# A four-layer graph network on one core: the third layer's gather pass as a pipeline of pairs of tiles

## The reference

```python
h = h_dir * h_mag                                  # one row of 256 per node
scores = h[src] @ a_s + h[tgt] @ a_t               # one number per edge
mx = maximum(segment_max(scores, tgt), -1e9)
ex = exp(scores - mx[tgt]);  se = segment_sum(ex, tgt)
agg = segment_sum(h[src] * (ex / (se[tgt] + 1e-10)), tgt)
```

## Time and profile before

| what | us |
|---|---|
| median of 3 runs | 4127.81 (4125.18 to 4128.53) |
| span of the profiled execution, first to last instruction | 4145.4 |
| the third layer's gather pass, first gather to last addition | 1642.65 to 2325.15 |

### The profile page before, as it was taken

How to read it: one execution, slowest core, us unless ns; L and a number is a source line. 1 busy time by engine, 2 the same in 40 slices (tenths; PEclk the granted TensorE clock), 3 DMA queues, 4 the chain that set the end, 5 groups by cost and what they waited for, 6 DMA issues and landing times. The chain is left out here.

```text
span 4145.4 us, 56575 instructions
## 1 busy us (share of the span) xinstructions
PE 2931.3 (71%) x12389; PEld 2013.0 (49%) x12389; DVE 2921.6 (70%) x6934; ACT 1927.7 (47%) x5796; POOL 2507.2 (60%) x2316
## 2 busy tenths in 40 slices
PE   4566566266777795467666587888888878888884
PEld 3444444144444463344444335666665446666662
DVE  3455555577777754355555648999999759999997
ACT  3444444211111133222223446878787348888884
POOL 5666664366666301666666048888886268888881
PEclk7667777578888896666767799999999999999997
DMA  5655444366666421344434249999997489999993
GB/s 158 136 135 132 133 135 105 121 187 202 200 201 193 154 92 53 106 114 114 113 111 110 41 151 225 223 219 223 219 224 180 139 200 223 226 222 226 225 222 104
DMA packets 363228, 673.24 MB, mean 162 GB/s; under 512 B 65028, under 2 KB 167413, under 8 KB 362910
## 3 DMA queue, kind: packets, MB, share of 16 engines
q0 software_dynamic: 160896, 403.63, 43.2%
q1 hardware_dynamic: 197902, 262.18, 19.4%
q10 hardware_dynamic: 4112, 3.83, 0.3%
HBM read 579.68 MB, written 89.74 MB: 161 GB/s over the span
## 5 line engine op out<-in xcount | busy, mean ns | idle before, releaser
L1850 POOL DMA_INDIRECT t_kv<-kv_tab,srcT x440 | 713.0, 1620 | 152.7 <-issue 130.7
L2053 PE MATMUL bank<-t_kv,t_oh 128*128 128x260 f32 x1760 | 519.8, 404 | 144.6 <-DVE acc L1921 68.3
L1410 POOL DMA_INDIRECT grow<-h_tab,srcT x440 | 417.1, 948 | 297.7 <-issue 98.1
L533 POOL DMA_INDIRECT grow<-h_tab,srcT x440 | 418.0, 950 | 251.6 <-issue 110.7
L878 POOL DMA_INDIRECT grow<-x_tab,srcU x416 | 394.3, 948 | 245.7 <-issue 109.4
L1846 POOL DMA_INDIRECT t_kv<-kv_tab,srcT x440 | 456.4, 1037 | 134.1 <-issue 123.1
L1013 PE MATMUL bank<-grow,oh 128*128 128x272 f32 x832 | 324.7, 497 | 195.1 <-DVE acc L931 107.8
L2022 PE MATMUL bank<-we,t_aT 128*128 128x256 f32 x1760 | 436.4, 388 | 24.1 <-DMA t_aT<-attrT_tab 21.0
L2003 ACT ACTIVATE t_kv<-t_kv 128x64 f32<-128x64 f32 x1696 | 445.2, 333 | 0.0
L2053 PEld LDWEIGHTS bank<-t_kv,t_oh 128*128 128x128 f32 x1760 | 284.8, 191 | 261.1 <-issue 150.5
L2034 PE MATMUL bank<-H,t_ohT 128*128 x2640 | 367.5, 276 | 18.8 <-DVE t_ks L1884 18.4
(11 more groups left out here) (406 smaller groups left out, 5611.5 us busy)
## 6 DMA issues: line engine op xcount, KB each, us to landing
t_aT<-attrT_tab SPq DMA_DIRECT2D x110, 512.0 KB
H<-in_edge_attr SPq DMA_DIRECT2D x440, 64.0 KB
attrT_tab<-H SPq DMA_DIRECT2D x55, 512.0 KB
t_ohT<-place_tab SPq DMA_DIRECT2D x110, 256.0 KB
H<-lo_tab SPq DMA_DIRECT2D x55, 256.0 KB
grow<-h_tab,srcT POOLq DMA_INDIRECT x880
place_tab<-H SPq DMA_DIRECT2D x55, 256.0 KB
wbig<-place_tab SPq DMA_DIRECT2D x55, 256.0 KB
```

The costliest lines, as they stand in the source:

```text
L533: nc.gpsimd.indirect_dma_start(out=grow[:, t % RA, :], out_offset=None, in_=h_tab, in_offset=bass.IndirectOffsetOnAxis(ap=srcT[:, t:t + 1] ...
L1410: nc.gpsimd.indirect_dma_start(out=grow[:, t % R2, :], out_offset=None, in_=h2_tab, in_offset=bass.IndirectOffsetOnAxis(ap=srcT[:, t:t + 1 ...
L1850: nc.gpsimd.indirect_dma_start(out=kv[:, u, :], out_offset=None, in_=kv_tab, in_offset=row, compute_op=ALU.add).then_inc(g_ready[u], 16)
L2053: nc.tensor.matmul(PS[4 + t % WIN3][:, 0:LHW], oh[:, t % OHS, :], kv[:, t % UB, F:KVW], start=True, stop=True).then_inc(products, 1)
```

## The change

The slots are replaced by STEPS2 = 220 + 13 + 1 steps, one for each pair of tiles, on DVE, ACT and PE. In step p:

- PE multiplies pair q = p - 13, then does at most one softmax part, then (p % 4 == 1) the terms of a group.
- DVE does the scores of a group (p % 4 == 0), at most one softmax part, then adds pair r = p - 14, then takes the factor and rescales (one step in eight), then makes one-hots (p % 4 == 3).
- ACT weighs pair p - 12, one step ahead of PE.

The softmax of batch b begins when its last scores are there, at step 8(b + 1), with PE's part k at step 8(b + 1) + k and DVE's one step later.

Two tiles of a pair are summed in PSUM. The first product of pair r opens a bank (`start=True`), the second adds to it (`start=False`), unless the second tile lies in another block: then it goes to the bank of the next pair, which that pair's first product has opened before. `turn_i`, made once in the start-up, holds 0 or 1 for this, and PE reads it into registers, four for every four pairs (`turns`). The last pair of a batch always has a second bank of its own. So there are 248 additions in the place of 440. Three banks rotate (WINS = 3) in the place of four. A block gets at least two tiles in the start-up's counts. POOL's waits count pairs. The wait for the rescaling has been moved from behind `rescale` to ahead of the first addition of the next batch. `iota_r` and `first0` live shorter, and the PSUM banks are one tensor with the same addresses.

```diff
+PAIRS = ET // 2
+PB = NB // 2
+WINS = 3
+def last_of_batch(r):
+    return r % PB == PB - 1 or r == PAIRS - 1
+def window_no(r):
+    return r // PB * (PB + 1) + r % PB
+def pairs_behind(t):
+    return t // 2 if t % 2 == 0 and t // 2 % PB else t // 2 + 1
...
+        def window_by_turn(first, r, turn, width):
+            here, there = r % PB % WINS, (r % PB + 1) % WINS
+            two = BANKS[:, first + here:first + there + 1, :] if here < there else BANKS[:, first:first + WINS, :][:, ::-2, :]
+            return two[:, ds(turn, 1), 0:width].rearrange("p a c -> p (a c)")
...
+                        step(nc.vector.tensor_scalar(n_b[:, 0:NT], n_b[:, 0:NT], 2.0, None, ALU.max))
...
+                        dve.wait_ge(starts_in, 32)
+                        nc.vector.tensor_tensor(turn_i[:, :], block_i[0:1, 1:ET:2], block_i[0:1, 0:ET:2], ALU.not_equal)
...
-        WIN2 = 4
+        LAG2 = 13
+        STEPS2 = PAIRS + LAG2 + 1
...
-                                pool.wait_ge(products, t - R2 + 1)
+                                pool.wait_ge(products, pairs_behind(t - R2))
...
+                        def add_to(block_of, bank, number):
+                            if number > 0:
+                                dve.wait_ge(added, number)
                             window = acc[:, ds(block_of, 1), 0:F + 1].rearrange("p a c -> p (a c)")
-                            nc.vector.tensor_tensor(window, window, PS[2 + t % WIN2][:, 0:F + 1], ALU.add).then_inc(added, 1)
+                            nc.vector.tensor_tensor(window, window, bank, ALU.add).then_inc(added, 1)
+                        def add_window(r, blocks):
+                            dve.wait_ge(products, r + 1)
+                            if r % PB == 0:
+                                dve.wait_ge(sm.rescaled, r // PB + 1)
+                            add_to(blocks[2 * r % HB], window_of(2, r, F + 1), window_no(r))
+                            if last_of_batch(r):
+                                add_to(blocks[2 * r % HB + 1], own_window_of(2, r, F + 1), window_no(r) + 1)
...
+                        for p in range(STEPS2):
+                            r = p - LAG2 - 1
+                            if p % 4 == 0 and 0 < p <= PAIRS:
+                                scores(p // 4 - 1)
+                            for k in range(4):
+                                b = softmax_of(p, k + 1)
+                                if b is not None:
+                                    sm.dve(dve, step, b, k)
+                            if r >= 0:
+                                if r % 4 == 0:
+                                    blocks = following
+                                add_window(r, blocks)
...
+                            if p % 4 == 3 and 1 <= (p - 11) // 4 < NH:
+                                one_hots((p - 11) // 4)
...
+                            q = p - LAG2 + 1
+                            if 0 <= q < PAIRS:
+                                for t in range(2 * q, 2 * q + 2):
+                                    row = grow[:, t % R2, 0:F + 1]
+                                    nc.scalar.activation(row, row, ACT.Copy, scale=w[:, q // PB % 2, t % NB:t % NB + 1]).then_inc(rows_ready, 1)
...
+                        def first(r):
+                            t, n = 2 * r, window_no(r)
+                            if t % HB == 0:
+                                pe.wait_ge(oh_ready, t // HB + 1)
+                            pe.wait_ge(rows_ready, t + 1)
+                            if n >= WINS:
+                                pe.wait_ge(added, n - WINS + 1)
+                            nc.tensor.matmul(window_of(2, r, F + 1), oh[:, t // HB % 2, t % HB, :], grow[:, t % R2, 0:F + 1], start=True, stop=True, skip_group_check=True)
...
+                        for p in range(STEPS2):
+                            q = p - LAG2
+                            if 0 <= q < PAIRS:
+                                if q % 4 == 0:
+                                    turn = turns(q, 4)
+                                if q % PB == 0:
+                                    first(q)
+                                if not last_of_batch(q):
+                                    first(q + 1)
+                                second(q, turn[q % 4])
+                            for k, part in ((0, 0), (1, 1), (2, 2), (3, 3), (4, 5)):
+                                b = softmax_of(p, k)
+                                if b is not None:
+                                    sm.pe(pe, b, part, sums_done, min(NH, 2 * b + 2))
+                            if p % 4 == 1 and p // 4 < NH:
+                                terms(p // 4)
```

More of the change, by code:

```diff
@@ L131, in graph_layers, with window_of, own_window_of @@
         we = sb("we", [ED, F])
-        PS = [ctx.enter_context(nc.psum_tensor(f"bank{i}", [P, 512], F32)) for i in range(8)]
+        BANKS = ctx.enter_context(nc.psum_tensor("bank", [P, 8, 512], F32))
+        PS = [BANKS[:, i, :] for i in range(8)]
         accf = acc[:, :, :].rearrange("p a b -> p (a b)")
+        def window_of(first, r, width):
+            return BANKS[:, first + r % PB % WINS, 0:width]
+        def own_window_of(first, r, width):
+            return BANKS[:, first + (r % PB + 1) % WINS, 0:width]
+        def window_by_turn(first, r, turn, width):
+            here, there = r % PB % WINS, (r % PB + 1) % WINS
+            two = BANKS[:, first + here:first + there + 1, :] if here < there else BANKS[:, first:first + WINS, :][:, ::-2, :]
+            return two[:, ds(turn, 1), 0:width].rearrange("p a c -> p (a c)")
         def ds(start, n):
@@ L155, in tile_ints, with turns @@
                                                             skip_runtime_bounds_check_because="made from the sorted destinations")[1]
+        def turns(r0, n):
+            return nc.values_load_multi_w_load_instructions(turn_i[0:1, r0:r0 + n], engines=[mybir.EngineType.PE], min_val=0, max_val=1,
+                                                            skip_runtime_bounds_check_because="a comparison's result")[1]
         def last_ints(n, top):
@@ L1270, in _ @@
                         split3(step, 1)
-        PAIRS = ET // 2
         LAG = 11
@@ new lines, in second @@
+                        def second(r, turn):
+                            t, n = 2 * r + 1, window_no(r) + 1
+                            pe.wait_ge(rows_ready, t + 1)
+                            rows_of, ones_of = grow[:, t % R2, 0:F + 1], oh[:, t // HB % 2, t % HB, :]
+                            if last_of_batch(r):
+                                pe.wait_ge(added, n - WINS + 1)
+                                nc.tensor.matmul(own_window_of(2, r, F + 1), ones_of, rows_of, start=True, stop=True, skip_group_check=True).then_inc(products, 1)
+                            else:
+                                nc.tensor.matmul(window_by_turn(2, r, turn, F + 1), ones_of, rows_of, start=False, stop=True, skip_group_check=True).then_inc(products, 1)
```

89 lines of the change are left out of this document (25 added, 64 removed).

## The result

The changed kernel takes 4140.15 us (median of 13 runs, 4137.10 to 4152.86); the kernel before, measured beside it, 4128.53 us (13 runs, 4117.11 to 4136.44). The ratio is 1.0028, with a 95% interval of 1.002 to 1.0036: **slower by 0.28%**, about 12 us, where 4056 was forecast.

The account below looks back on a forecast made before the run. Waits were taken to bound the pass, no engine being full: late reports stop DVE, the scores, PE, then POOL. Flow -57, ring -9.3, tail -6 and start-up +0.5 gave -72 us, 4056; range 4020 to 4110.

Parts of the forecast that it names:

- Late reports: Exchanges of PE with DVE: lateness costs PE 2.0 us a group, so a group takes 10.6 us.
- 50 x 1.14 = 57 us: Flow behind the ring's filling: 50 groups take 10.6 us each in the place of 11.74, -57 us.
- rival A: Gather pass: POOL alone bounds, all its other waits go, -104 us, 4024; chance 0.27.
- upper bound of 13.5: Time of a group in the flow if each has the worst lateness: 8.6 + 4.9 us.
- PE per group, 8.6 us: PE's work for eight tiles: 8.05 us plus 0.59 for one added load, under POOL's 10.03.
- DVE: DVE in the pass: 192 additions fall away, 81 us of its 346; no bound before or after.
- ACT runs ahead: ACT's list in the pass: it runs ahead with 189 us of work in all.
- Ring full, -9.3: POOL's first long wait, when the ring of 40 is full, goes whole: -9.3 us.
- Tail, -6: From last gather to last addition: 31 us in the place of 37.6, -6, between 0 and -15.
- Clock: PE's granted clock in the pass, 0.72 on average; the skill's section speaks against a gain from it.
- B: Rival: only the ends gain, flow keeps 11.4 to 11.74 us a group, -15 to -32, 4104; chance 0.17.
- C: Rival: slower through the handshake of three banks between PE and DVE, 13.0 us a group, +48, 4176; chance 0.10.

Follow-up runs that it names:

- e1: Changed kernel with the third layer's products streaming 129 of 257 columns: 4139.15 us, kernel before 4143.79.
- e4: Changed kernel with four window banks in the place of three: 4155.77 us, kernel before 4143.79, ratio 1.0034.
- e11: Changed kernel without the softmax of the third layer's pass, constant weights: 4127.53 us, kernel before 4152.89 (one run).
- e7: Changed kernel with the factor's exponential moved behind the weighing in ACT's list: 4124.76 us, kernel before 4133.97, ratio 0.9982.
- e10: Kernel of e7 with a one-column memset on POOL behind each gather: 4145.94 us, kernel before 4145.27, ratio 1.0001.
- e12: Kernel of e5 with the factor's exponential behind the weighing, as in e7: 3908.05 us, kernel before 4152.89 (one run).
- e5: Changed kernel with plain DMAs from POOL in place of the third layer's indirect gathers (wrong rows): 3925.05 us, kernel before 4133.97.
- e15: Changed kernel with indirect gathers always of the same 128 neighbouring rows: 4163.73 us, kernel before 4152.89 (one run).
- e9: Changed kernel with every second gather of the third layer's pass a plain DMA: 3948.15 us, kernel before 4145.27.
- e3: Changed kernel with three more 128 x 128 identity products on PE in every step: 4238.8 us, kernel before 4143.79.

## Why the prediction was wrong

**The step that failed is "Late reports": 2.0 us a group taken as PE's loss on top of 8.6 us of work, which gave 10.6 us a group.** It made the lateness something that is paid once a group and that a better order could take beside other work. The flow stayed at 11.75 us a group, with PE busy for 7.6 of them (419.7 / 55), and the term of 50 x 1.14 = 57 us was worth nothing. The runs show in its place a lateness that comes with POOL's gathers in the indirect form and limits the flow by itself: whether PE has half the work (e1), a fourth bank (e4) or no softmax at all (e11), the flow is 1.44 to 1.50 us a gather, 11.5 to 12.0 us a group; with plain DMAs, or every second one plain, no report is late and the group takes 7.7 to 8.4 us. By what path a gather delays a report stays open. POOL's 10.03 us a group, the lower bound of the prediction and the whole of rival A, was reached by no version with indirect gathers alone.

Two readings were at hand. The first and the second layer's gather passes of the kernel before, which are other code, have nearly the same step: 51.7 to 698.8 us for 440 gathers (L533) and 784.7 to 1403.6 for 416 (L878) are 1.47 and 1.49 us each. And the "4.9 us late" of the earlier trace rows is how long DVE stood, not how late the report was: SP took the terms, done at 1783.71, at 1789.21, 5.5 us later, and the longest delay in that pass is 14.8 us by the semaphores' records. It was not the worst case that the upper bound of 13.5 took it for.

- *PE per group, 8.6 us:* not the bound, as said, and e1 confirms it. The load of `turn_i` was put at 0.59; the trace of the changed kernel has it at 0.33. PE's busy time in the flow went down by 27 us, to 7.6 us a group over the pass.
- *DVE:* 248 additions and 70 us less busy time came as worked out, and brought nothing, also as said.
- *"ACT runs ahead":* wrong. In the new list the factor's exponential waits ahead of the next weighing, one step ahead of PE. Before, ACT waited for the factor too (L1345, 315.1 us), but PE waited for weighed rows for 2.0 us only the earlier trace rows; now for 33.1. What that is worth in time is less sure: against 1.0028, e7's ratio makes it 19 us and that of e10, with the same move, 11. e12 against e5 shows it without late reports. It is the likeliest reason that the changed kernel is slower and not equal, but no run beside the changed kernel shows it.
- *Ring full, -9.3:* the first product came 40.1 us after the first gather, inside the 33 to 47 forecast, but the ring's wait shrank only from 9.61 to 6.46 us. The second half of this first pair, in the timeline of the changed kernel:

```profile
1677.16 1.06 PE L1580 MATMUL bank<-grow,oh 128*128 128x257 f32 x2
```

  It was done at 1678.22, and POOL, whose 41st gather needs nothing else, went on at 1691.52, 13.3 us later, when it had stood for 6.5 us. Worth 3, not 9.
- *Tail, -6:* the last addition ends at 2314.65, 37.0 us after the last gather, as against 37.6: nearly nothing.
- *Clock:* taken as it was, 0.72; measured 0.73. The Trainium skill's warning ("TensorE: Matmul & The Clock Gate", section "A second HAM failure mode: psum-queue depth-cycling") agrees with a clock this low, but tells nothing of the change, which left it where it was; four banks (e4) had 0.70.
- *Rivals.* B had the flow right (11.4 to 11.74 us, lateness untouched by the change), but its gains at the ends were 3 us and less than 1, not 15. C had the sign right and the reason wrong: e4 shows no gain from a fourth bank. No rival asked what else stands ahead of the weighing in ACT's new list.
- *A small slip:* (1691.48 - 1642.65) / 39 is 1.252, not 1.253; it moves no result.

What stays open is where the 12 us of the result lie: in the two profiled executions the pass is even 3 us shorter after (679.5 us from first gather to last addition, before 682.5), while the medians of 13 runs differ by 12 us the other way. The profiled run of before lies 17 us above its median, so this pair can't place the 12 us. The start-up's +0.5 is far below that.

## What to carry to other kernels

When an engine's waits end under names that have nothing to do with them, ask what else was under way each time, and replace that by a cheap stand-in before planning an order around the lateness; e5 would have told more than any sum. Then split what the stand-in brings into the waits that it removes and the work that it makes cheaper. If passes of different code run at the same step, as three did here, suspect what they share before their order. An engine's own time per item, 1.25 us here, is a bound that may be out of reach. And when work is moved to run ahead, look at each small instruction that stays in front of it in its list.

## What was not expected of the hardware

- PE's reports come late while POOL issues indirect gathers of 128 rows of 1032 bytes every 1.25 us: 5.1 us behind the terms of e11 (1900.69 to 1905.76), 13.3 us in the fill of the changed kernel's ring. DVE's and ACT's don't. Many come only when POOL stands, 2.7 and 3.3 us after the start of its last gather in e1 and e11; but a stop is not needed (1978 to 1986 us in the changed kernel, where 46 of the 136 late ones came while POOL had issued without a stop since the recorded end), and in the ring's fill POOL stood for 6.5 us first. By what path a gather delays a report, no run shows; scattered rows (e15) are ruled out, and so are the bytes and the software queue by themselves (e5).
- It is far weaker in the fourth layer, where indirect gathers are issued as well, 31 in 50 us, and POOL's waits are 4.3 and 1.2 us: in that pass of the kernel before 36 of PE's 732 recorded reports lie over 1 us behind, 2.5 us at most. The gathers of every second pair add to their destination there, and the rows are wider. Which of these matters was not tried.
- The traces lack many semaphore records where indirect gathers run: in the changed kernel's pass they have 423 for 696 recorded ends of DVE, in e5's, with plain DMAs, 691 for 691.
- Every second gather plain is enough (e9: 8.4 us a group, no late report).
- A memset of 0.11 us between two gathers leaves them 1.25 us apart, since POOL has 0.30 us to the next anyway (e10).
- Fewer columns per product brought a lower clock: 0.52 with 129, 0.73 with 257 (e1); three more products a step raised it to 0.83 (e3).
